# One raise after each half of TensorE's period in an attention over gathered neighbours: two semaphores instead of four, and the further visits behind the scores

## What is computed

```python
Q = einsum('nf,hfd->hnd', x, Wq);  K = ... Wk;  V = ... Wv
s = einsum('hef,hef->eh', Q[:, receiver], K[:, sender]) * scale
m = segment_max(s, receiver);  p = exp(s - m[receiver])
alpha = p / segment_sum(p, receiver)[receiver]
msg = alpha.T[:, :, None] * V[:, sender]
agg = segment_sum(msg, receiver)
x = layernorm(x + (x + nan_to_num(agg.mean(axis=0)) @ Wout))
```

## Time and profile before

| | us |
|---|---|
| median of 3 runs | 3332.77 |
| lowest, highest | 3322.11, 3349.67 |
| profiled execution | span 3320.5 |
| PE busy in the span | 2315.6 (70%) |
| POOL busy | 1926.4 (58%) |
| DVE busy | 1768.0 (53%) |
| ACT busy | 1302.5 (39%) |

### The profile page before, as it was taken

The page is one execution under the profiler, slowest core; times in us unless marked ns, Lnnn a source line. Parts: engine busy times, 40 slices in busy tenths (PEclk is TensorE's granted clock), DMA queues, the critical chain, the costliest instruction groups (busy, mean ns, idle before and its releaser), DMA issues.

```text
span 3320.5 us, 65724 instructions
## 1 busy us (share of the span) xinstructions
PE 2315.6 (70%) x18911; PEld 1708.5 (51%) x18912; DVE 1768.0 (53%) x6022; ACT 1302.5 (39%) x3789; POOL 1926.4 (58%) x2644
## 2 busy tenths in 40 slices
PE   3878878657676667766676676775667676767775
PEld 2767767534444445544454454554445444545545
DVE  7988878744444444444444444444444444444457
ACT  3444444343333434333333333343333333333333
POOL 3777777745566565555555556565555565555630
PEclk9999998565566656566657656566655656655667
DMA  4766765101111111111111111111111111111100
GB/s 128 223 207 210 214 204 170 32 16 35 25 35 37 28 36 35 29 35 28 34 29 34 35 29 35 28 35 36 29 35 35 26 35 27 34 27 35 29 15 21
DMA packets 175708, 196.91 MB, mean 59 GB/s; under 512 B 95203, under 2 KB 97939, under 8 KB 173265
## 3 DMA queue, kind: packets, MB, share of 16 engines
q1 hardware_dynamic: 125078, 138.90, 15.2%
q0 software_dynamic: 50048, 51.35, 8.2%
HBM read 184.87 MB, written 5.25 MB: 57 GB/s over the span
## 4 chain that ended last, share of the span: by engine, by line
PE 30%; another core or an unknown queue 23%; issue 20%; DVE 16%; ACT 5%; DVEq 3%; POOL 2%; ACTq 1%; POOLq 0%; DMA 0%; SPq 0%
PE psS L1410 7%; PE psV L1369 5%; PE psM L1369 4%; PE psT L1364 3%; DVE O L817 3%; PE psM L1245 2%; PE psN L1245 2%; DVE nm_old L899 2%; DVE rmax L886 2%; DVE l_st L814 1%; PE psV L1236 1%; PE psX L1236 1%; ACT XT L1100 1%; PE psX L1359 1%
## 5 line engine op out<-in xcount | busy, mean ns | idle before, releaser
L528 POOL DMA_INDIRECT XS<-x_dram,dst_bs x1564 | 1487.5, 951 | 1088.6 <-DVE O L817 624.8
L814 DVE SCALAR_TENSOR_TENSOR l_st<-l_st,alpha,rsum 64x1 f32 x782 | 168.5, 215 | 768.8 <-remote 636.2
L1369 PE MATMUL psV<-XS,PT 128*128 128x64 f32 x1568 | 327.2, 380 | 327.6 <-ACT PT L1144 165.0
L1369 PE MATMUL psM<-XS,dst_bs 128*128 128x64 f32 x1560 | 328.9, 384 | 310.0 <-ACT dst_bs L1144 176.6
L1369 PEld LDWEIGHTS psV<-XS,PT 128*128 128x128 f32 x1568 | 313.7, 296 | 360.1 <-ACT PT L1144 187.9
L1369 PEld LDWEIGHTS psM<-XS,dst_bs 128*128 128x128 f32 x1560 | 316.5, 300 | 338.5 <-ACT dst_bs L1144 194.8
L886 DVE TENSOR_REDUCE rmax<-psS 128x1 f32<-128x512 f32 x391 | 270.5, 692 | 397.2 <-remote 345.1
L1410 PE MATMUL psS<-XT,Ubuf 96*128 96x512 f32 x522 | 463.5, 987 | 18.4 <-issue 7.5
L1144 ACT COPY PT<-psT 128x512 f32<-128x512 f32 x196 | 114.9, 586 | 642.3 <-remote 527.0
L1144 ACT COPY dst_bs<-psT 128x512 f32<-128x512 f32 x195 | 114.3, 586 | 558.3 <-remote 474.7
L1410 PE MATMUL psS<-dst_bs,Ubuf 96*128 96x512 f32 x260 | 229.8, 983 | 12.9 <-issue 9.3
(11 more groups left out here) (280 smaller groups left out, 4311.8 us busy)
## 6 DMA issues: line engine op xcount, KB each, us to landing
big<-in_edge_attr_2x SPq DMA_DIRECT2D x195, 512.0 KB, 4.3
big<-dst_turned SPq DMA_DIRECT2D x49, 512.0 KB
XS<-x_dram,dst_bs POOLq DMA_INDIRECT x1564
O<-codes_dram SPq DMA_DIRECT2D x200, 6.0 KB
x_dram<-x SPq DMA_DIRECT2D x12, 128.0 KB, 1.9
out<-big SPq DMA_DIRECT2D x12, 128.0 KB
codes_dram<-O SPq DMA_DIRECT2D x3, 384.0 KB
big<-in_src SPq DMA_DIRECT2D x1, 768.0 KB
```

The costliest lines, as they stand in the source:

```text
L528: pool.indirect_dma_start(xs(k, j), None, x1_dram, bass.IndirectOffsetOnAxis(ap=idx2[b % SB][:, k * CPP + j:k * CPP + j + 1], axis=0)).the ...
L814: dve.scalar_tensor_tensor(out=ls, in0=ls, scalar=al[half], in1=rs[half], op0=ALU.mult, op1=ALU.add)
L1369: last = pe.matmul(ps, pt[:, j * P:(j + 1) * P], xs(k, j), start=(j == 0), stop=(j == CPP - 1))
```

## The change

PE raises `first_half` once, after the last of what the first half of the period has (turned rows, then weighing), and `second_half` once, after the last of the second (turned probabilities, then scores). ACT's copy of turned rows and DVE's update both wait for `first_half`; ACT's copy of turned probabilities and DVE's maximum wait for `second_half`, with counts shifted so that each waits for the same period's work as before. The further visits move behind the scores. Matmuls, their number and the other semaphores stay.

```diff
-            for s, n in ((s_done, 2), (nm_kept, 3), (pv_done, 4), (nm_taken, 2), (cur_done, 2), (tp_done, 2), (exp_done, 3), (pt_done, 4),
+            for s, n in ((second_half, 1), (nm_kept, 3), (nm_taken, 2), (cur_done, 2), (exp_done, 3), (pt_done, 4),
...
                 if on(2):
                     now = columns(col_r[(J - 2) % 6])
-                    dve.wait_ge(s_done, vv)
+                    dve.wait_ge(second_half, m if isinstance(m, int) else dve.snap(vv - 1, min_val=H2))
                     dve.tensor_reduce(rmax[:, q:q + 1], psSc[q][:, :], AX_X, ALU.max)
                 if on(4):
-                    dve.wait_ge(pv_done, vv)
+                    dve.wait_ge(first_half, vv)
...
                 if on(0):
-                    act.wait_ge(tx_done, vv)
+                    act.wait_ge(first_half, vv)
                     take_rows(XT[J % 3], a)
                     take_U(Ubuf[a], cols, u_done)
                 if on(2):
-                    act.wait_ge(tp_done, vv)
+                    act.wait_ge(second_half, m + 2 if isinstance(m, int) else act.snap(vv + 1, min_val=H2 + 2))
                     act.copy(PTs[a][:, :], psT[:, :]).then_inc(pt_done, 1)
...
-                    turn_rows(J % S2, a)
+                    first = turn_rows(J % S2, a)
                 if on(4):
                     pe.wait_ge(pt_done, vv)
-                    weigh((J - 4) % S2, PTs[a], psVc[a][:, 0:D], pv_done)
+                    first = weigh((J - 4) % S2, PTs[a], psVc[a][:, 0:D])
+                first.then_inc(first_half, 1)
                 if on(3):
                     pe.wait_ge(exp_done, vv)
-                    turn_probs(Pms[1 - a], psT, tp_done)
-                    further_visits(J - 3)
+                    second = turn_probs(Pms[1 - a], psT)
                 if on(1):
                     pe.wait_ge(mask_done, vv)
                     pe.wait_ge(u_done, vv)
-                    pe.matmul(psSc[1 - a][:, :], Ubuf[1 - a][:, :], XT[(J - 1) % 3][:, :], start=True, stop=True).then_inc(s_done, 1)
+                    second = pe.matmul(psSc[1 - a][:, :], Ubuf[1 - a][:, :], XT[(J - 1) % 3][:, :], start=True, stop=True)
+                if on(3) or on(1):
+                    second.then_inc(second_half, 1)
+                if on(3):
+                    further_visits(J - 3)
```

More of the change, by code:

```diff
@@ L235, in gnn_resnorm_kernel @@
         xg = [sem(f"x1_gathered{k}") for k in range(S2)]
-        (tx_done, s_done, mask_done, u_done, tp_done, pt_done, pv_done, upd,
+        (first_half, second_half, mask_done, u_done, pt_done, upd,
          cur_done, exp_done, al_done, nm_kept, nm_taken) = (
-            sem(n) for n in ("tx_done", "s_done", "mask_done", "u_done", "tp_done", "pt_done",
-                             "pv_done", "upd", "cur_done", "exp_done", "al_done", "nm_kept", "nm_taken"))
+            sem(n) for n in ("turned_and_weighed", "probs_turned_and_scored", "mask_done", "u_done", "pt_done",
+                             "upd", "cur_done", "exp_done", "al_done", "nm_kept", "nm_taken"))
         (x_mask, x_u, x_s, x_max, x_nm, x_cur, x_kept, x_exp, x_tp, x_pt, x_pv, x_upd) = (
@@ L1359, in turn_rows, with turn_probs, weigh @@
                     last = pe.transpose(psXc[b][:, j * P:(j + 1) * P], two, ident[:, :])
-                last.then_inc(tx_done, 1)
-            def turn_probs(probs, ps, done):
+                return last
+            def turn_probs(probs, ps):
                 for j in range(CPP):
                     last = pe.transpose(ps[:, j * P:(j + 1) * P], probs[:, j * P:(j + 1) * P], ident[:, :])
-                last.then_inc(done, 1)
-            def weigh(k, pt, ps, done):
+                return last
+            def weigh(k, pt, ps):
                 for j in range(CPP):
                     last = pe.matmul(ps, pt[:, j * P:(j + 1) * P], xs(k, j), start=(j == 0), stop=(j == CPP - 1))
-                last.then_inc(done, 1)
+                return last
             def further_visits(J):
@@ L1381, in further_visits @@
                         pe.sem_inc(turn_steps, 1)
-                        turn_probs(PmX, psA, x_tp)
+                        turn_probs(PmX, psA).then_inc(x_tp, 1)
                         pe.wait_ge(x_pt, xx)
-                        weigh(J % S2, PTX, psA[:, 0:D], x_pv)
+                        weigh(J % S2, PTX, psA[:, 0:D]).then_inc(x_pv, 1)
                         pe.reg_add(xv, xv, 1)
```

## The result

| | before | changed |
|---|---|---|
| median of 4 runs, us | 3334.22 | 3445.69 |
| lowest, highest | 3322.11, 3349.67 | 3430.21, 3468.38 |
| profiled execution, span | 3320.5 | 3428.1 |
| granted clock, mean | 0.674 | 0.648 |

The ratio is 1.0339, 95% interval 1.0306 to 1.0372: the change made the kernel slower by 3.4%, 111 us. I had forecast 3301 us with a range of 3130 to 3405. The time lies above the range, on the side of the third rival.

What follows compares the result with a forecast made beforehand. The kernel was taken to pace itself: gather runs hold PE's raises until POOL stops for O. Terms 0 + 0 + 0 + 5 - 37 = -32 us, counted on the median 3332.8, gave 3301 us, range 3130 to 3405.

Steps and rivals of the forecast that it cites:

- third rival: Scores slip behind the free window, so copy and weighing fall into POOL's pause: +86 us, 3387 us, chance 0.25.
- Term (1): Two PE raises fewer a period: taken as 0, against an estimate of 20 us from the skill's 26 ns tail.
- Term (2): ACT's copy of turned rows (L1100) waits for the weighing behind them: cost 0.
- Term (4): Eleven further visits moved behind the scores on PE: between -25 and +21 us, taken as +5.
- until POOL stops: Reading that a run of gathers lets about one period's raises through, then holds PE's raises until POOL stops for O.
- free window: Start of a gather run, when PE's raises still pass: taken to let one period through, so a run holds two chunks.
- term (3): ACT's copy of turned probabilities (L1144) waits for the scores: 0 to 176 us (0.45 us a period), taken as 0.
- Term (5): Queue of held raises: window unchanged, held raises 0.76 us apart, fewer of them saves 0 to 111 us, taken as -37.
- a count in raises: Rival that the free window counts PE's raises, so runs hold three chunks: 3188 us, chance 0.33.
- a count in matmuls: Forecast's own case that the free window measures PE's work, 24 to 26 matmuls, unchanged by the change: chance 0.42.

Runs made afterwards that it cites:

- e17: Kernel before with a rest of 1.24 us on POOL after each chunk's gathers, in a job with holds: 3172.18 us, ratio 0.951.
- e15: Kernel before with ten raises a period instead of four, the six extra ones waited for by nobody, with holds: 3307.42 us, ratio 0.9951.
- e5: Kernel before with ten raises a period instead of four, in a job without holds: 2718.92 us, ratio 1.0007.
- e10: Kernel before with ten raises a period instead of four, in another job without holds: 2717.98 us, ratio 0.9995.
- e2: Kernel before with only the first half merged, one raise for turned rows and weighing, with holds: 3331.49 us, ratio 0.9998.
- e1: Kernel before with only the further visits moved behind the scores, four raises a period, with holds: 3336.39 us, ratio 1.0018.
- e14: Kernel before with only the further visits moved behind the scores, measured once more with holds: 3339.53 us, ratio 1.0028.
- e4: Kernel before with visits moved and ACT's copy of turned probabilities also waiting for the scores, four raises kept, with holds: 3424.41 us, ratio 1.029.
- e13: Kernel before with visits moved and ACT's copy of turned probabilities also waiting for the scores, four raises, another job with holds: 3410.36 us, ratio 1.0263.
- e9: The changed kernel itself, run beside the kernel before in a job without holds: 2772.4 us against 2720.11, ratio 1.0195.
- e16: Kernel before with the weighing put ahead of the turning of rows in PE's period, with holds: 3332.91 us, ratio 1.0009.
- e18: Changed kernel with PE turning the rows three times over, 20 matmuls a period instead of 16, with holds: 3369.65 us, ratio 1.0095 to the kernel before.
- e6: Kernel before with a rest on POOL after each chunk's gathers, in a job without holds: 3171.79 us, ratio 1.1667.
- e8: Kernel before without the raise of turn_steps by PE's sequencer that nobody waits for, without holds: 2717.11 us, ratio 0.9994.
- e12: Kernel before with PE turning the rows three times over, 20 matmuls a period instead of 16, without holds: 2714.65 us, ratio 0.9976.

## Why the prediction was wrong

**What held.** PE's raises are held where POOL's gathers run back to back, and POOL stops because O is late: e17 takes away both at once. Term (1), raises as such cost nothing: e15, e5, e10. Term (2), the copy of turned rows behind the weighing, 0: e2. Term (4), moved visits, +5 taken: 6 and 9 us measured over the kernel before, in e1 and e14, with intervals that begin at 0.9999 and 1.0004.

**What did not hold in the reading of the rows** is that a run holds PE's raises "until POOL stops". In the very run of the earlier trace rows the answer at 714.89 came while POOL gathered on:
```profile
713.83 0.95 POOL L528 DMA_INDIRECT XS<-x_dram,dst_bs  x1 [0.30 <-issue]
715.08 0.95 POOL L528 DMA_INDIRECT XS<-x_dram,dst_bs  x1 [0.30 <-issue]
...
721.33 0.94 POOL L528 DMA_INDIRECT XS<-x_dram,dst_bs  x1 [0.31 <-issue]
726.79 0.95 POOL L528 DMA_INDIRECT XS<-x_dram,dst_bs  x1 [4.51 <-DVE O L817]
```
In the attention of the kernel before, 140 of the waits of DVE's L814 that are marked remote are over 0.3 us, and 29 of them ended inside a run of gathers. So "one chunk for the raise released in the pause and one for that in the free window" fits the 103 runs of two chunks, not the 42 of three and the 41 of one.

**The step that failed is term (3)**, ACT's copy of turned probabilities behind the scores. I had its size, 0.45 us a period and 176 us from above, and took 0 with the words that the weighing in the earlier trace rows "is held until 1529.69 in any case". That was one period, chosen from the kind in which the slack exists. The runs give 78 to 90 us for this wait alone (e4 and e13 less e1 and e14), 0.20 to 0.23 us for each of 391 periods, about half of my upper bound. The 0.45 us is right for a period in which nothing is held: in e9's rows the copy leaves PE 0.25 us idle before the weighing at 1446.48, and takes away the 0.20 us by which the weighing overlaps the turning of rows. In all of e9 the matmuls of the weighing wait 0.20 us a period for the copy, its weight loads 0.44 us.

**By which way it gets to the end is argued, not shown.** The picture of my third rival occurs: the hold falls between the turned probabilities and the scores, and then copy, weighing and update stand in POOL's pause (the rows at 1551 to 1565). I had priced that case at 3387 us, 59 us under the measured time, with an own range to 3450, so the mechanism was named and its price too low. My price counted longer pauses alone. In fact the pauses are also more, 214 instead of 192, and more runs end after one chunk, 80 instead of 41. Yet the moved visits alone have nearly as many pauses with a weighing inside and cost almost nothing, so the share of this way stays open. A second way, less granted clock for a PE that waits for the copy (0.58 instead of 0.62), is not borne out: e15 and e16 have a lower and a higher clock than the kernel before at about its time.

**Term (5)**, -37 us, failed too. Remote waits did fall by 332 us in all, but they fell on ACT and DVE, where they were replaced by waits for the scores; POOL's wait for O, the only one that the time hangs on, rose. The 0.75 us for each raise held singly was also misread. In the stretch of the earlier trace rows DVE makes its mask (L808) from 963.66 to 964.14, before L886, and 0.48 of the 0.76 us is that. The semaphores' own events in the trace give the pause of the earlier trace rows as 1517.38 for the weighing and 1518.12, 1518.16 and 1518.20 for the other three: behind the first, a raise more is 0.04 us. How the window is measured stays open; a count in raises is excluded by e15, a count in matmuls made doubtful by e18.

**The range** was drawn to the middle of the third case instead of its end. A case with a quarter of the chance, and with the only price of the sum that had been set to zero against a bound of 176 us, should have been let in whole.

## What to carry to other kernels

A raise that is bundled with a later instruction's makes every reader of the earlier one wait; look whether that reader's work lay beside the later instruction and now stands behind it, on the engine's own chain. Here 0.59 us of ACT, hidden beside the scores until then, cost 2.4 to 2.7% of the change's 3.4%, and the two raises saved gave nothing. When a term is taken as zero because "it waits anyway", check that also on the periods where it does not wait. And when a reading says that something lasts until another thing stops, look for a case in which it ended sooner; here it stood in the rows already shown.

## What the runs showed of the hardware

- The same kernel took 3330 us in some jobs and 2720 in others, on the same two chips. The difference goes with the held raises: without them no wait is marked remote, POOL's pauses fall from 667.5 us to 7.6 (e10), and the gathers run at 5.05 us a chunk, near my floor of 5.0. What decides which kind a job is was not found. The fastest version depends on it: the kernel with rests is the best of all with holds (0.951) and the worst without (1.167), so it can't simply be recommended.
- In e17 and e6 DVE's mask of chunk m took 0.91 and 0.95 us on average instead of 0.49 in the kernel before, where POOL's memset of 1300 columns ran in each period. POOL still waited only 3.6 us (e17) for O, so it lay off the path.
- Held raises come out together: of PE's raises in the attention of the kernel before, 354 followed the one before them within 0.1 us (2 in e8, without holds).
- Four useless matmul records a period raised the mean granted clock from 0.72 to 0.82 (e12 against e10) and the kernel became 0.2% faster, not slower. With holds, kernels at 0.58 (e15), 0.61 (before) and 0.65 (e16) from 1000 to 3000 us took 0.995, 1 and 1.001 of the time.
